# The last feed-forward group of four batches becomes two groups of two, in a repeating step whose order is rewritten

## What is computed

```python
x = x + tanh(g_xattn) * cross_attention(layernorm(x), context)
h = layernorm(x)                       # then two layers, per batch:
for l in range(2):
    q, k, v = split(shift_token(h) @ wqkv[l])          # 8 heads of 64
    q, k = rotary(l2norm(q) * qs, l2norm(k) * ks)
    h = h + local_attention(q, k, v) @ wo[l]           # window 64
    t = layernorm(shift_token(h)) @ w1[l] + b1[l]
    a, g = split(t)                                    # 341 each
    h = h + (a * gelu(g)) @ w2[l] + b2[l]
x = x + tanh(g_ffn) * h
```

## Time and profile before

| what | value |
|---|---|
| median of 3 runs (lowest to highest) | 407.94 us (407.48 to 408.99) |
| time of the profiled execution | 406.78 us |
| its span, first to last instruction | 405.0 us |
| mean granted TensorE clock | 0.974 |
| busy: PE, DVE, ACT, POOL | 351.5, 328.6, 306.7, 236.3 us |
| chain that ended last, by engine | DVE 33%, ACT 30%, PE 24%, issue 8%, POOL 3%, DMA 2% |

### The profile page before, as it was taken

One profiled execution on the slowest core, in us unless ns is written; L12 is line 12 of the kernel. 1 busy time (PEld: TensorE's weight loads), 2 busy tenths in 40 slices (PEclk: granted clock), 3 DMA queues, 4 the chain that ended last, 5 costly groups with the idle time before them and its releaser, 6 DMA issues.

```text
span 405.0 us, 8128 instructions
## 1 busy us (share of the span) xinstructions
PE 351.5 (87%) x2480; PEld 259.5 (64%) x2480; DVE 328.6 (81%) x1279; ACT 306.7 (76%) x969; POOL 236.3 (58%) x260
## 2 busy tenths in 40 slices
PE   2886789999989899899989998998899989987874
PEld 1665577778667666677666765686577667665531
DVE  3958789999869999699969996999699879965434
ACT  3687579898997689967897689768976896688550
POOL 2297888887546796555656565655565546662200
PEclk9958889999999999999999999999999999999998
DMA  8900000000000000000000000000000000000000
GB/s 221 328 4 0 1 2 0 3 2 0 2 2 0 2 1 2 1 2 2 1 2 2 2 2 0 2 1 2 1 2 2 2 26 2 2 2 27 0 28 26
DMA packets 3327, 7.14 MB, mean 18 GB/s; under 512 B 386, under 2 KB 1700, under 8 KB 3284
## 3 DMA queue, kind: packets, MB, share of 16 engines
q1 hardware_dynamic: 2861, 6.13, 4.5%
q0 software_dynamic: 144, 0.26, 0.4%
q10 hardware_dynamic: 279, 0.22, 0.2%
HBM read 5.57 MB, written 1.05 MB: 16 GB/s over the span
## 4 chain that ended last, share of the span: by engine, by line
DVE 33%; ACT 30%; PE 24%; issue 8%; POOL 3%; DMA 2%; SPq 0%; POOLq 0%; DVEq 0%
ACT pp L981 9%; DVE pp L1260 7%; DVE sn L1242 5%; PE ps L761 4%; DVE cs L1239 4%; PE ps L675 4%; ACT gl L1009 3%; DVE ss L1249 3%; ACT pT L986 3%; DVE wqkv_raw L1293 2%; ACT L1078 2%; ACT L1052 2%; PE ps L712 2%; PE ps L701 2%; ACT sqr L969 2%
## 5 line engine op out<-in xcount | busy, mean ns | idle before, releaser
L981 ACT ACTIVATE pp<-pp,nm 128x128 f32<-128x128 f32 x256 | 99.0, 390 | 1.8 <-DVE nm L1260 1.2
L389 POOL TENSOR_TENSOR pp<-pp,pri 128x512 f32<-128x512 f32 x64 | 66.4, 1040 | 42.0 <-DVE pri L1267 41.0
L396 POOL TENSOR_TENSOR cs<-cs,sn 128x512 f32<-128x512 f32 x64 | 81.2, 1284 | 0.0
L403 POOL TENSOR_TENSOR cs<-cs,rr 128x512 f32<-128x512 f32 x32 | 33.4, 1043 | 68.3 <-ACT rr L975 68.3
L1260 DVE CUSTOM_DVE_ANT_0 pp<-ps,msk,rr 128x128 f32<-128x128 f32 x256 | 72.3, 347 | 0.0
L1239 DVE TENSOR_TENSOR cs<-ps,ctab 128x512 f32<-128x512 f32 x64 | 43.1, 674 | 22.5 <-ACT sqr L969 22.4
L969 ACT ACTIVATE sqr<-ps 128x512 f32<-128x512 f32 x64 | 37.5, 587 | 27.2 <-PE ps L493 27.1
L491 PE MATMUL ps<-wqkv_hi,h_hi 128*128 128x512 f32 x96 | 55.0, 573 | 0.1
L981 ACT ACTIVATION_READ_ACCUMULATOR pp<-pp,nm 128x1 f32 x256 | 48.5, 189 | 0.0
L675 PE MATMUL ps<-pT,vv 128*64 128x128 f32 x512 | 35.0, 278 | 14.8 <-ACT pT L986 14.8
L1242 DVE TENSOR_TENSOR sn<-ps,stab 128x256 f32<-128x256 f32 x128 | 47.7, 414 | 0.0
(11 more groups left out here) (129 smaller groups left out, 709.0 us busy)
## 6 DMA issues: line engine op xcount, KB each, us to landing
wqkv_raw<-in_L_ffn_wqkv_dram SPq DMA_DIRECT2D x2, 768.0 KB, 12.3
out_dram<-xt SPq DMA_DIRECT2D x4, 256.0 KB, 2.4
w_raw<-in_w_dram SPq DMA_DIRECT2D x1, 682.0 KB, 11.7
xt<-in_x_dram SPq DMA_DIRECT2D x1, 512.0 KB, 8.8
wo_raw<-in_wo_dram SPq DMA_DIRECT2D x1, 512.0 KB
xt<-in_x_dram SPq DMA_DIRECT2D x1, 384.0 KB, 5.8
ct<-in_ctx_dram SPq DMA_DIRECT2D x1, 360.0 KB, 10.2
ct<-in_ctx_dram SPq DMA_DIRECT2D x1, 270.0 KB, 6.5
```

Of the source, the lines that this page charges most:

```text
L389: T(pp[m.j][:, a, :, :], pp[m.j][:, a, :, :], pri[m.j][:, a * 4:a * 4 + 4].unsqueeze(2).to_broadcast([128, PAIRS, 128]), ALU.mult).then_in ...
L396: T(cs[m.j][:, part], cs[m.j][:, part], sn[m.j][:, part], ALU.add).then_inc((aq_done, ak_done)[s], 1)
L981: A(pp[m.j][:, a, c, :], pp[m.j][:, a, c, :], ACT.Exp, bias=nm[m.j][:, a * 4 + c:a * 4 + c + 1], scale=-1.0, accum_out=psum_[m.j][:, a * 4 ...
```

## The change

1. Groups 0 to 6 stay groups of four (`GT = 7`); the last four batches become group 7 (batches 28 and 29) and group 8 (batches 30 and 31), of 256 columns each. Their calls stand as single jobs `s.n == ...`, their banks are second and third entries of the bank tuples, and each has its own DMA.
2. The order in every engine's step is another, with other banks for group and pair jobs and other `passed` waits. PE: `rows_k(n+2)`, `project_v(n+1)`, `project_q(n+4)`, `rows_q(n+2)`, `out_proj(n)`, `scores_(n+2)`, `weights_T(n+1,0)`, `weights_T(n+1,1)`, `project_k(n+5)`, `attend(n+1)`, with group jobs between `project_v` and `scores_`. DVE: `maxima_(n+1,0)`, `turns(n+3,q)`, `maxima_(n+1,1)`, `turns(n+4,k)`, `squared(n+3,q)`, `inverse(n+1,0)`, `k_rows(n+2)`, `v_rows(n+1)`, `inverse(n+1,1)`, `squared(n+4,k)`, `attn_residual(n)`. `final_T` and `result` move one step later, from the GELU step into the value step, `group_high` and `group_low` too.
3. Pairs 0 and 1 and the weight casts around them are placed anew (n from -168); the casts of layer 1's weights move from step -7 to step 7.

```diff
+GT = 7
-        HA_B, HG_B = (TK, TQ, VB), (TK, SB, VB)
-        ACC_B, FT_B, DEV_B, VAR_B = SB, QB, VB, OB
+        HA_B, HG_B = ((SB, OB, VB), (QB, TQ, SB), (VB, QB, OB)), ((TQ, TK, OB), (VB, OB, TQ), (KB, OB, TQ))
+        ACC_B, FT_B, DEV_B, VAR_B = (KB, SB, TQ), (TK, KB, VB), (KB, QB, KB), (TK, SB, VB)
+        class Group:
+            def __init__(self, g):
+                first = GB * g if g < GT else GB * GT + (g - GT) * 2
+                self.layer, self.b = first // B, first % B
+                self.size = GB if g < GT else 2
+                self.end = first + self.size
+                self.at = slice(self.b, self.b + self.size)
+                self.w = slice(0, self.size * N)
+                self.k = max(g - GT + 1, 0)
...
             def project_k(m):
+                passed(f_upd, 2 * groups_by(m.i - 9))
+                passed(gl_ready[2], groups_by(m.i - 7))
+                passed(hn_ready, groups_by(m.i - 6))
                 passed(tk_done, min(m.i, ALL))
...
             def deviation(g):
-                mm(ps[:, DEV_B, :], cen[:], xs[:, b:b + GB, 0:N], start=True, stop=True).then_inc(m_ps, 1)
+                if g < GT:
+                    n = GB * g + GB
+                    passed(f_upd, 2 * groups_by(n - 5))
+                    passed(tk_done, min(n + 5, ALL))
+                mm(ps[:, DEV_B[o.k], o.w], cen[:], xs[:, o.at, 0:N], start=True, stop=True).then_inc(m_ps, 1)
...
             def back(g, c):
+                if c == 0 and g < GT:
                     n = GB * g + GB + 3
-                    passed(gl_ready[1], groups_by(n - 3))
-                    passed(nm_done[1], min(n + 2, ALL))
+                    passed(gl_ready[2], groups_by(n - 3))
+                    passed(tk_done, min(n + 5, ALL))
```

More of the change, by code:

```diff
@@ L770, in final_T @@
+                o = Group(g)
+                for i in range(o.size):
+                    last = tr(ps[:, FT_B[o.k], i * 128:(i + 1) * 128], stg[:, i, :], idn[:])
                 last.then_inc(f_T, 1)
             def step(s):
+                if s.n == 40:
+                    passed(hn_ready, 9)
+                    final_T(7)
+                if s.n == 35:
+                    back(7, 1)
                 if s.n == -3:
-                    passed(x_res, 4)
+                    passed(x_pT, 2)
@@ L795, in step @@
+                if s.n == -5:
+                    passed(x_res, 4)
+                if s.pair(10) is not None:
+                    query_in(s.pair(10))
+                if s.n == 34:
+                    passed(u_ready[2], 7)
+                    variance(8)
                 if s.on(0):
@@ L1027, in step @@
+                if s.n == -73:
+                    norms(0)
+                if s.n == -49:
+                    tokens_affine(0)
+                if s.on(2):
+                    q_rows(s.at(2))
+                if s.n == 30:
+                    dev_square(7)
+                if s.n == -13:
+                    probs_out(1)
+                if s.n == 49:
+                    dev_rstd(8)
+                if s.on(3):
+                    lengths(s.at(3))
+                if s.n == 7:
                     weights_high(1, 0)
@@ L1375, in step @@
[L1375 to L1386 removed]
+                if s.n == -3:
+                    w1_in(0)
@@ L1397, in step @@
-                if s.n == -5:
-                    bias_sum()
+                if s.n == 33:
+                    gate(7, 2)
+                if s.group(-3) is not None:
+                    gate(s.group(-3), 2)
+                if s.n == 46:
+                    result(8)
+                if s.n == -13:
+                    token_high(0)
+                if s.n == -24:
+                    context_normed(1)
+                if s.n == -17:
+                    maxima(1)
+                if s.n == 13:
+                    w1_in(1)
@@ L1400, in _ @@
+                if s.n == -43:
+                    tokens_normed(0)
+                if s.n == 43:
+                    update(8)
             pipeline(step)
```

797 lines of the change are left out of this document (436 added, 361 removed).

## The result

| | before | after |
|---|---|---|
| median of 5 runs | 408.59 us (407.48 to 409.04) | 397.23 us (396.82 to 404.87) |
| ratio after / before | | 0.9733, 95% interval 0.9706 to 0.9761 |
| profiled execution: time, span | 406.78, 405.0 us | 399.71, 397.9 us |

The kernel is 2.7% faster. The forecast was 391, its range 385 to 404. The profiled execution of after is 2.5 us slower than its median run, the one of before 1.8 faster than its own, so the two spans differ by only 7.1 where the medians differ by 11.4. (Of nine executions of this kernel, with the four of e1, five took 394.9 to 399.7 us and four 401.7 to 404.9; what is longer in one of the four is shown under e1.) The forecast's own range, 386 to 396, is missed; the stated one holds because it takes in the rivals.

The account below looks back on a forecast made before the run. With no engine full, waits were taken to close the step, PE being nearest its limit. Terms -11.4, -2.0, -2.6, -3.7 and fill 0 sum to -19.7, giving 388.2; a 3.1 allowance made 391 us, range 385 to 404 (own 386 to 396).

Parts of the forecast that it names:

- The bound: Repeating step: no engine full, waits close it; PE busy 38.64 of 41.86 us a round, order gives at most 3.2.
- The GELU step: Step with the GELUs, where ACT's ring of waits holds `attend`: 9.98 us instead of 11.57.
- (c): ACT issues `gelu(g,1)` and the second table load after both `weights_out`: 0.6 + 1.28 us off what `attend` waits for.
- (a): ACT runs `weights(n+1,0)` before `heads_out(n)`, so it no longer waits for `attend` before four exponentials; no separate size.
- (b): PE issues `scores_(n+2)` before both `weights_T`, DVE starts with `maxima_(n+1,0)`, so exponentials find input ready; no separate size.
- a round of 39.3: Four repeating steps placed at 9.35, 9.98, 9.80 and 10.15 us, with 38.1 of PE work; 41.7 before.
- Steps 8 to 27: Middle stretch: four rounds of 39.3 and one of 40.0, 197.2 us against 208.6, so -11.4.
- The allowance of 0.1 a step: Whole run: 3.1 us added because a hand placement is too smooth, some ten places having under 0.3 to spare.
- The fill: Stretch up to batch 0's `attend`, with POOL's jobs reordered: change of 0 us, bounds -2 and +4.
- The end: Last `attend` to the end, with the last group split into 256 columns: 20.2 us against 23.9, so -3.7.
- The table load: Two more loads at the end, 1.28 us each; a cited drain of about 1.38 per switch left out.
- Rival 3: Fill grows by 4 us from POOL's four early jobs and PE's low clock: 397 us, chance 0.09.

Follow-up runs that it names:

- e1: The changed kernel run once more, unchanged, as a control: median 401.77 us of four (394.86 to 402.11).
- e9: Changed kernel with `attend` doing all even heads first and waiting for the second half of the weights only in its middle: 403.45 us, ratio 0.9867 to before.
- e10: Changed kernel with `attend` doing all even heads, then all odd ones, both waits still at its head: 406.53 us, ratio 0.9946 to before.
- e3: Changed kernel with `gelu(g,1)` and the second table load put back in front of both `weights_out`: 408.52 us, ratio 0.9963 to before.
- e7: Changed kernel with `weights_T(n+1,0)` ahead of `scores_(n+2)` in all steps but the GELU step: 399.82 us, ratio 0.9725 to before.
- e4: Changed kernel with the eight `token_high` casts done by ACT behind `results` instead of by DVE: 399.69 us, ratio 0.9773 to before.
- e8: Changed kernel with the edits of e7 and e4 together: 401.54 us, ratio 0.9794 to before.
- e11: e9 with the third weight part's cast and subtraction moved back into the early fill: 402.22 us, ratio 0.9841 to before.
- e2: Changed kernel with the last four batches left as one group (GT = 8): 402.67 us, ratio 0.9858 to before.

## Why the prediction was right in sign and size, and where its steps failed

- **The bound.** Right. No engine was full, and waits closed the step; now PE is 64% of the chain, its rows cover 39.18 of 40.02 in a round, and e9 against e10 shows for three steps of four that what PE waits, the kernel waits.
- **The GELU step.** Right: placed at 9.98, 10.04 measured, and e3 gives it back whole (11.52) by undoing (c) alone: 9.4 us of the kernel's time.
- **(a) `heads_out` and (b) `scores_`.** (a) is worth some 6 us, more in the first eight steps than I had given it. Of (b) only PE's half was taken back: with DVE's half left in, that costs 58 us. What (b) adds to the kernel before, no run shows. Each move was taken back alone, out of the new order, so the three prices don't add up to the gain.
- **The failed step: a round of 39.3, made of 38.1 of PE work and 1.2 of waits.** It is 40.02, and the term that was too small is the waits. The busy time alone says the opposite, work up from 38.64 to 39.18 and 0.84 of waits, but it covers short waits, as the rows above show. Counted from start to start instead, against the shortest distance between the same two jobs in steps 8 to 27 of these profiles, PE waits about 2.0 us in this round: 0.3 in front of each of three `attend`s, 0.7 in the deviation step (forecast 0.48) and, `attend` apart, 0.3 in the value step (forecast 0.06). That leaves about 38.0 of work. The same count gives some 38.2 of work and 3.7 of waits before (all of these are estimates from the timelines, good to 0.2 or so). So PE's work hardly changed.
- **The 38.1 was right by luck.** I took 0.5 off a busy time that held as much in hidden waits. The 0.5 itself was wrong: I had read the earlier trace rows as a price of the projection, 0.80 behind wide matmuls and 0.50 behind short ones. It is only where its row begins. The rows below show the GELU step. Before, the six wide ones last 2.28 from start to start (283.87 to 286.15) and the projection pass behind them 0.64 (to 286.79), together 2.92. After, they last 2.67 (284.23 to 286.90), and the pass, now elsewhere, 0.32: 2.99. Nothing was saved. PE's timeline, before and then after:

```profile
283.87 2.84 PE L712 MATMUL ps<-hn,w1g 128*128 128x512 f32 x6
...
286.79 0.40 PE L492 MATMUL ps<-wqkv_lo,h_hi 128*128 128x512 f32 x1
```

```profile
284.23 2.74 PE L730 MATMUL ps<-hn,w1g 128*85 128x512 f32 x6
286.90 1.16 PE L661 MATMUL ps<-kT,qT 64*128 64x128 f32 x16
```

- **The wait at `attend`.** I gave it 0.05 to 0.15. In after ACT's second `weights_out` ends about when PE's last pass does (289.78 in ACT's timeline), and the hand-over of 0.25 is the wait. From the start of that pass to `attend` it takes 0.63, in e9, which doesn't wait there, 0.33: 0.3 a step. In e7 more lead changes it little.
- **Steps 8 to 27.** -6.4 for -11.4: the five rounds take 40.31, 41.05, 40.19, 40.02 and 40.66, where I had four of 39.3 and one of 40.0. Most of it is the 0.7 of each round; about one more lies in the value step of the round from 12 (11.3 for 10.3), where DVE's `w1_in(1)`, moved from step 19 to step 13, ends at 208.3, half a us ahead of it, and a value input waits 0.87 for `turns`. The allowance of 0.1 a step covered 2 of the 5 us.
- **The fill.** The forecast 0, with a bound of +4, was the second miss: +6.0 in the first profile, +1.3 to +6.6 in the profiles with `attend` unchanged, against the first one of before. Of the causes that I had named, the clock is one part: 0.67 goes with 1.6 to 3.9 us. The other 3.2 to 4.6 lie between `scores_(0)` and `attend(0)`, where the new order puts `rows_q(1)` behind a wait for the pair's exponentials. The long cast is real but hidden: with it gone (e4, e8) nothing is gained, in e11 another wait takes its place. The wait for the pair's exponentials stands in no profile of before at this place. That a kernel of the new order with this wait moved regains 3 us was not tried, and why the clock is lower in some executions stays open.
- **A term that was at nothing: the held cast.** The forecast gave the casts of `token_high` no change. In three profiles of the new order the last one takes 4.0 in place of 0.26, and with the fall of the clock behind it steps 8 and 9 are 5.3 us longer in e1 than in after. It isn't in the profile of after, so not in the table, but an execution that has it keeps some 5 us less of the gain.
- **The end.** -3.7 forecast, -3.4 measured, the 256-wide prices within 0.02 (GELU 0.47, two updates 1.00). The extra loads were free but for the middle one, as placed. e2 adds that the split was worth 7.5 at the end in this order: the sum was right for two effects that I had not told apart, which is luck in part.
- **The table load.** The rule that I cited, the Trainium skill (ScalarE: Activation LUTs, "What ACT_TABLE_LOAD costs"), adds 1.38 us to a switch. Here the operation behind a load starts 0.02 after its end in both kernels: 286.27 behind 284.97 + 1.28, 385.64 behind 384.34 + 1.28. The measurement decides: leaving it out was right.
- **The rivals.** None came true whole. Rival 3, a longer fill, is in the result, with a price beside a smaller gain in the steps. Added up in the profile, the stretches miss by 12.6 us, 6.0 in the fill and 5.0 in steps 8 to 27; the allowance of 3.1 took up part of it.

## What to carry to other kernels

When an order written by hand is changed, count an engine's work as start-to-start time of both neighbours: a longer operation behind wide matmuls may be the end of the wide ones, and moves with them instead of vanishing. Don't take PE's busy time for its work: set the start-to-start time of a job beside that of the same job elsewhere, and the short waits show. Once an engine's rows fill a step, look at its wait for the last hand-over, but check what the cure does to the engine's own pipelining before splitting a batch of matmuls. And price the fill by its landmarks in several profiles: in a fill that varies by 3 us with the clock, neither a gain nor a loss of that size is seen in one. A long record that costs nothing in one place can cost 5 us in another; follow it in every profile, and in the executions that are longer than the rest.

## What the runs showed of the hardware

- Sixteen matmuls of 128 x 64 by 128 columns take 1.09 us when their outputs alternate between the two halves of the partitions, and 1.55 to 1.58 when eight of one half stand in a row. The Trainium skill (TensorEngine Tiling (Array Packing), "Performance Considerations") names a left side of up to 64 columns as a case for two-fold column tiling; that the order of issue changes the time by 0.46 us is what e10 adds.
- A DVE cast of 128 x 256 fp32 from SBUF to SBUF took 3.60 us for 0.28, held over three POOL instructions. It was as long again in e2 (3.60) and e7 (3.45), 0.67 in e1 and 1.03 in e9. In the fill it cost nothing that could be measured. The last cast took 4.05 in e1 and e3 and 4.04 in e9, and there PE waited 2.60 behind it, its granted clock fell from 1.00 to between 0.59 and 0.73 for the ten us around and behind the wait, and two steps together took 5.3 us more in e1.
- PE's busy time covers waits of 0.2 to 0.3 us: the same eight transposes are busy 1.09 whether the next matmul starts 0.85 or 1.14 after them.
- A table load costs 1.28 us, with no gap of over 0.02 behind it in any row shown here.
